# A one-core Mamba block with two adapters: the gate projection and the state sum change places in the pipeline, and the adapters' first projections use four column groups

## The reference, cut to what matters

```python
# 1. adapted projection; A, Bm: the sequence's own rank-16 factors
h0 = x @ W.T + b + 2 * (x @ A) @ Bm
# 2. Mamba mixer, width D = 2048, state size N = 16
u, gate = split(h0 @ W_in.T)              # 2048 + 2048 columns
u = silu(conv4(u) + conv_b)
dt, Bm, Cm = split(u @ Wx.T)              # 64 + 16 + 16, each RMS-normalised
delta = softplus(dt @ Wdt.T + dt_bias)
state = exp(delta * A) * state + delta * u * Bm    # scan over the 256 tokens
y = ((state * Cm).sum(n) + u * D) * silu(gate)
x = x + y @ W_out.T
# 3. second adapted projection, then a mixture of 8 experts of rank 64, top 2
z = x @ base_W.T + base_b + (x @ A2) @ B2
w = top2(softmax(z @ gate_w.T))           # 8 logits for each token
x = x + sum_e w[:, e] * (z @ lora_A[e].T @ lora_B[e].T)
```

## Time and profile before

| | |
|---|---|
| median of three runs | 2683.88 us |
| the profiled execution's own time | 2682.71 us |
| its span | 2680.6 us |
| PE busy | 2405.3 us (90%), 10384 matmul records |
| DVE busy | 2245.6 us (84%) |
| POOL busy | 2118.3 us (79%) |
| ACT busy | 1696.4 us (63%) |
| chain that ended last, by engine | PE 52%, issue 14%, DVE 13%, POOL 10%, ACT 9% |
| DMA | 347.69 MB, mean 130 GB/s |

### The profile page before, as it was taken

How to read it: one execution, slowest core, us unless ns; L and a number is a source line. 1 busy time by engine, 2 the same in 40 slices (tenths; PEclk the granted TensorE clock), 3 DMA queues, 4 the chain that set the end, 5 groups by cost and what they waited for, 6 DMA issues and landing times.

```text
span 2680.6 us, 30841 instructions
## 1 busy us (share of the span) xinstructions
PE 2405.3 (90%) x10384; PEld 1943.0 (72%) x10384; DVE 2245.6 (84%) x2081; ACT 1696.4 (63%) x3754; POOL 2118.3 (79%) x1060
## 2 busy tenths in 40 slices
PE   8987998999989999899989999799989897677979
PEld 6866666677867877687867787688767776566767
DVE  0277788689898989989898989989999999889781
ACT  1366656675677656776577756776577756775450
POOL 0086778689798988989798978898889997999770
PEclk9988999999999999999999999999999998898989
DMA  5452442543354334544244434543345322532331
GB/s 194 124 201 87 110 120 87 160 133 117 125 175 147 126 109 139 169 130 139 91 161 165 134 111 140 174 134 130 104 127 180 126 94 88 175 97 87 110 104 63
DMA packets 115531, 347.69 MB, mean 130 GB/s; under 512 B 21348, under 2 KB 28004, under 8 KB 113902
## 3 DMA queue, kind: packets, MB, share of 16 engines
q1 hardware_dynamic: 92618, 293.80, 33.8%
q10 hardware_dynamic: 22756, 51.92, 5.8%
HBM read 334.66 MB, written 11.02 MB: 129 GB/s over the span
## 4 chain that ended last, share of the span: by engine, by line
PE 52%; issue 14%; DVE 13%; POOL 10%; ACT 9%; ACTq 1%; DMA 0%; SPq 0%; POOLq 0%; DVEq 0%
PE gbank L589 9%; PE ubank L568 9%; DVE scan L1192 8%; PE late L631 6%; POOL st L1397 5%; DVE st L1204 4%; ACT scan L1036 4%; PE small L550 3%; PE late L667 3%; POOL st L1389 3%; PE late L597 3%; PE late L550 3%; ACT L1036 2%; PE small L747 2%; PE late L607 2%
## 5 line engine op out<-in xcount | busy, mean ns | idle before, releaser
L1192 DVE TENSOR_TENSOR_SCAN scan<-scan,st 128x1024 f32<-128x1024 f32 x512 | 1153.3, 2286 | 148.6 <-ACT scan L1036 121.0
L1389 POOL TENSOR_TENSOR st<-w_sb,bc 128x1024 f32<-128x1024 f32 x512 | 1197.2, 2357 | 101.0 <-PE late L597 66.2
L1036 ACT ACTIVATE scan<-delta,A_sb 128x255 f32<-128x255 f32 x2048 | 847.8, 459 | 1.8
L1397 POOL TENSOR_TENSOR st<-st 128x1024 f32<-128x1024 f32 x256 | 603.0, 2355 | 249.0 <-DVE st L1204 238.8
L589 PE MATMUL gbank<-h,wt 128*128 128x256 f32 x2048 | 470.4, 383 | 2.1 <-DMA wt<-in_W_in 2.1
L631 PE MATMUL late<-yg,wt 128*128 128x256 f32 x1792 | 408.6, 387 | 51.6 <-issue 51.6
L1204 DVE TENSOR_TENSOR st<-scan,bc 128x1024 f32<-128x1024 f32 x384 | 453.2, 1208 | 0.0
L589 PEld LDWEIGHTS gbank<-h,wt 128*128 128x128 f32 x2048 | 385.7, 190 | 76.3 <-issue 26.1
L631 PEld LDWEIGHTS late<-yg,wt 128*128 128x128 f32 x1792 | 346.0, 194 | 109.1 <-issue 60.9
L568 PE MATMUL ubank<-h,wt 128*128 128x256 f32 x1712 | 419.6, 402 | 1.3 <-ACT u_sb L903 1.1
L568 PEld LDWEIGHTS ubank<-h,wt 128*128 128x128 f32 x1712 | 350.9, 205 | 59.0 <-ACT u_sb L903 3.0
(11 more groups left out here) (192 smaller groups left out, 2597.2 us busy)
## 6 DMA issues: line engine op xcount, KB each, us to landing
wt<-in_W_in SPq DMA_DIRECT2D x256, 512.0 KB, 3.9
wt<-in_W_out SPq DMA_DIRECT2D x128, 512.0 KB, 3.4
wt<-in_cond_W SPq DMA_DIRECT2D x64, 512.0 KB, 3.7
bc<-bc_rows ACTq DMA_DIRECT2D x64, 512.0 KB, 6.9
wt<-G_tiles SPq DMA_DIRECT2D x32, 512.0 KB, 3.6
wt<-in_ffn_B SPq DMA_DIRECT2D x32, 512.0 KB, 3.4
xb<-in_x SPq DMA_DIRECT2D x8, 1024.0 KB, 5.7
x<-in_x ACTq DMA_DIRECT2D x28, 256.0 KB, 4.0
```

Source lines behind the costliest of these rows:

```text
L1036: last = fn(t[:, k, 1:T], delta[:, c, 1:T], ACT.Exp, scale=A_sb[:, col:col + 1])
L1192: v_.tensor_tensor_scan(Tps[q % 2][:, :], Tps[q % 2][:, :], x_, 0.0, ALU.mult, ALU.add).then_inc(scan_done, 1)
L1389: tt(st[:, n % ST_RING, :, :], w_sb[:, i % 2:i % 2 + 1, :].to_broadcast([P, NQ, T]), bc[:, 0, q * NQ:(q + 1) * NQ, :], ALU.mult).then_inc( ...
L1397: tt(st[:, n % ST_RING, :, :], st[:, n % ST_RING, :, :], st[:, (n - 1) % ST_RING, :, :], ALU.add).then_inc(add_done, 1)
```

## The change

Eight things change, and nothing in what is computed.

1. PE order: `gate_chunk(i+1)` goes to the end of slot i and `sum_states(i-1)` to the start of slot i.
2. The state sum moves from bank late to bank gbank. It waits for the silu of gate i (`q_done`); gate i+1 waits for `y_gate(i-1)`; the folded products of batch 0 (`g`, `b2`, `bias`) wait for `y_gate(i-1)` too. Late jobs no longer wait for `y_gate`.
3. DVE order: `y_sum` and `y_gate` go behind scan 3; `norm` and the first part of softmax stand around scan 2.
4. The jobs of h0 are spread: single chunks in c = 0, 2, 4, 6, 8, 10, two in c = 11, and `la` of sequence b+3 in c = 14. The last `g` job goes to slot 15.
5. Adapters: factor A is padded to 32 columns; part k goes to column group k % 4, so that a bank holds four partial sums on 128 partitions; all 128 rows are copied, and the second factor, held four times at partitions 0, 32, 64, 96 (zeros between), sums them in its matmul.
6. The gate's folded matrix becomes columns 16 to 23 of the second adapter's A, so the logits come from `la2` alone: two matmuls instead of eighteen.
7. Softplus and `delta_add` work on each dt job (two chunks) as it comes, not on pairs.
8. ACT loads a table that holds Exp and Ln right after the gate's silu; dt evacuations all come after `decay(i,3)`.

```diff
@@ late and last jobs, tiles
+    if c == 14 and b + 3 < B:
+        return ("la", b + 3, 0)
...
-        if c == 0:
-            return ("la", j, 0)
-        if c in (1, 3, 5, 6):
-            return ("cond", j, (1, 3, 5, 6).index(c))
-        if c == 8:
-            return ("cond2", j, 4)
+        if c in (0, 2, 4, 6, 8, 10):
+            return ("cond", j, c // 2)
...
+        def softplus_of(i):
+            if i < 0:
+                return []
+            b, c = split(i)
+            if c == 14:
+                return [(b + 1, 0), (b + 1, 1)] if b < LAST else []
+            job = first_job(i)
+            return [job[1:]] if job and job[0] == "dt" else []
@@ SP
-                sp.dma_start(cB[:, :], cond_B[bass.ds(rA, 1)].rearrange("a r o -> r (a o)")).then_inc(cond_ld, 16)
+                for g in range(GR):
+                    sp.dma_start(cB[g * LRG:g * LRG + LR, :], cond_B[bass.ds(rA, 1)].rearrange("a r o -> r (a o)")
+                                 ).then_inc(cond_ld, 16)
@@ PE
                 for k in range(KH):
-                    last = mm(home(job)[0:LR, 0:T], cA[:, k, :], xb[:, k, :], start=(k == 0), stop=(k == KH - 1))
+                    g = k % GR * LRG
+                    last = mm(home(job)[g:g + LRG, 0:T], cA[:, k, :], xb[:, k, :], start=(k < GR), stop=(k >= GR))
...
             def gate_chunk(i):
-                if i:
-                    pe.wait_ge(q_done, i)
-                else:
+                if i == 0:
                     pe.wait_ge(pc_ev, KH + 2)
+                if i >= 2:
+                    pe.wait_ge(yg_done, i - 1)
...
             def sum_states(i):
                 pe.wait_ge(add_done, 3 * i + 3)
+                pe.wait_ge(q_done, min(i + 2, CHUNKS))
-                    last = mm(late[:, 0:T], ident[:, :], st[:, n % ST_RING, k, :], start=(k == 0), stop=(k == 1))
+                    last = mm(gbank[:, 0:T], ident[:, :], st[:, n % ST_RING, k, :], start=(k == 0), stop=(k == 1))
...
-            def logits(f, o):
+            def logits(o):
                 for tc in range(2):
                     tok = slice(tc * P, (tc + 1) * P)
-                    for k in range(KH):
-                        mm(o[:, tc * E:(tc + 1) * E], x_of(f)[:, k, tok], g_gate[:, k, :], start=(k == 0), stop=False)
-                    last = mm(o[:, tc * E:(tc + 1) * E], la2[:, tok], b2g[:, EG:EG + E], start=False, stop=True)
+                    last = mm(o[:, tc * E:(tc + 1) * E], la2[:, tok], b2g[:, EG:EG + E], start=True, stop=True)
...
+            gate_chunk(0)
             for i in range(CHUNKS):
-                gate_chunk(i)
+                if i:
+                    sum_states(i - 1)
                 if first_job(i):
                     run(first_job(i), i)
...
+                if i + 1 < CHUNKS:
+                    gate_chunk(i + 1)
@@ ACT
                 fn(qg[:, i % 2, :], gbank[:, 0:T], ACT.Silu).then_inc(q_done, 1)
-                if job and job[0] not in ("wb", "lg") and in_first_half(job):
+                fn_exp_table()
+                if job and job[0] == "ms":
                     evac(job)
                 decay(i, 2)
...
-                if i in SOFTPLUS_AT:
-                    softplus(*SOFTPLUS_AT[i])
+                for n, j in softplus_of(i):
+                    softplus(n, j)
@@ DVE
                 add_first(i)
+                if b and c == 9:
+                    soft_max_in(b - 1)
+                scan(i, 2)
+                if c == 13 and b < LAST:
+                    norm(b + 1)
+                scan(i, 3)
                 if i:
                     y_sum(i - 1)
...
                     y_gate(i - 1)
-                scan(i, 2)
-                scan(i, 3)
                 mul(i, 2)
                 mul(i, 3)
```

More of the change, by code:

```diff
@@ L25 @@
 LR = 16
+LRG = 32
+GR = P // LRG
 SLOTS = 32
@@ L177, in slot_tiles @@
 def slot_tiles(i):
-    tiles = [("gate", i, 0)]
+    tiles = []
     us = u_chunks(i)
@@ L195, in slot_tiles @@
         tiles += job_tiles(last_job(i))
-    return tiles
-PRO_TILES = [("cond", 0, m) for m in range(KH)] + [("u", v, 0) for v in range(NC)] + [("cond", 1, m) for m in range(4)]
+    if i + 1 < CHUNKS:
+        tiles += [("gate", i + 1, 0)]
+    return tiles
+PRO_TILES = [("cond", 0, m) for m in range(KH)] + [("u", v, 0) for v in range(NC)] + [("cond", 1, m) for m in range(4)] + [
+    ("gate", 0, 0)]
 TAIL_TILES = [("wo3", m, 0) for m in range(PAIRS)] + [("A", LAST, m) for m in range(EK)] + [
@@ L693, in run @@
                     pe.wait_ge(late_ev, LATE_NO[job])
+                    if LATE_NO[job] == 3:
+                        pe.wait_ge(pc_ev, 2 * KH)
+                if kind in ("g", "b2", "bias"):
                     pe.wait_ge(yg_done, i)
-                if kind in ("g", "b2", "bias"):
-                    pe.wait_ge(q_done, i + 1)
                 inc = done_inc(job)
@@ L879, in adapter @@
                 act.wait_ge(*made(job))
-                fn(la[:, :], home(job)[0:LR, 0:T], ACT.Copy, scale=2.0).then_inc(ev_inc(job), 1)
+                fn(la[:, :], home(job)[:, 0:T], ACT.Copy, scale=2.0).then_inc(ev_inc(job), 1)
             def cond_evac(o, j, m):
@@ L906, in x_evac @@
                 act.wait_ge(*made(job))
-                fn(sq[:, :], home(job)[0:RX, 0:T], ACT.Square, bias=one64[:, :]).then_inc(act_step, 1)
-                fn(xs[:, :], home(job)[0:RX, 0:T], ACT.Identity, bias=one64[:, :]).then_inc(ev_inc(job), 1)
+                fn(sq[:, :], home(job)[0:RX, 0:T], ACT.Square, bias=one64[0:RX, 0:1]).then_inc(act_step, 1)
+                fn(xs[:, :], home(job)[0:RX, 0:T], ACT.Identity, bias=one64[0:RX, 0:1]).then_inc(ev_inc(job), 1)
             def ms_evac(job):
@@ L986, in evac @@
                     act.wait_ge(*made(job))
-                    fn(la2[0:LR, :], o[0:LR, 0:T], ACT.Copy).then_inc(ev_inc(job), 1)
+                    fn(la2[:, :], o[:, 0:T], ACT.Identity, bias=one64[:, 1:2]).then_inc(ev_inc(job), 1)
                 elif kind == "A":
@@ L1037, in decay, with fn_exp_table @@
                 last.then_inc(dA_done, 1)
-            def in_first_half(job):
-                return not (job[0] == "dt" and job[2] % 2 == 0 and job[2] >= 2)
+            def fn_exp_table():
+                nc.scalar.preload_act_table_set("natural_log_exp_and_others")
             def softmax_exp(f):
@@ L1066, in _ @@
             softplus(0, 0)
+            softplus(0, 1)
             for q in range(Q):
@@ L1104, in _ @@
                     load_B(b + 1, 3)
-                if job and not in_first_half(job):
+                if job and job[0] in ("dt", "wT"):
                     evac(job)
+                for v in us:
+                    u_evac(v)
                 if i == 0:
@@ L1141, in _ @@
             act.wait_ge(t_la2, 1)
-            fn(la2[0:LR, :], small[0:LR, 0:T], ACT.Copy).then_inc(t_la2, 1)
+            fn(la2[:, :], small[:, 0:T], ACT.Identity, bias=one64[:, 1:2]).then_inc(t_la2, 1)
             for m in range(2):
```

137 lines of the change are left out of this document (61 added, 76 removed).

## The result

The changed kernel takes 2611.88 us (median of 4 runs, 2610.70 to 2612.61) against 2682.51 us of the kernel before on the same chip (2678.38 to 2684.15): ratio 0.9739, 95% interval 0.9722 to 0.9755, 70.6 us less. The forecast was 2608. The profiled execution has a span of 2609.9 us, PE busy 2321.2 (89%), DVE 2239.9 (86%), ACT 1622.4, POOL 2121.8, and 350.04 MB of DMA.

What follows compares the result with a forecast made beforehand. The prediction took DVE as the floor, with late PE orders in a handful of slots above it. Terms -43 - 6 + 4 - 20 - 7 - 4 = -76 on 2682.7 gave 2607, as median 2608 us; range for 8 in 10: 2585 to 2645.

Steps and rivals of the forecast that it cites:

- Batches 2 to 5, -43: Steady batches: 281.1 of DVE work, 11.0 of slot losses and 3.0 for the clock, 295.1 against 305.8, four times.
- c = 10, charged with 2.55: Steady batch, slot c = 10: a cond chunk beside two expert parts makes PE's loop 20.3, a loss of 2.55 us.
- c = 0 and 1, charged with 1.5: Steady batch: c = 0, heavy behind two expert jobs, was to lose 1.5 us.
- The late y pair costs nothing: DVE in each slot: y_sum behind scans 2 and 3 lets the gate start up to 1.25 us late at no cost.
- 1.25 us of free lateness: Each slot: the gate may start as late as 1.25 us into its own slot without delaying scan 2.
- Batch 0, -6: Batch 0: -9 from softplus without loads, +6 from g jobs waiting for y_gate, -3 in slots 14 and 15.
- Slot (1,0), 36: First slot of batch 1: bias, the moved g job, gate and ACT's loads of x lengthen it from 24 to about 36.
- Rival (a): Only the single stalls go, heavy slots keep their loss: 2634, up to 2650 with POOL's 2 a batch; chance 17%.
- Rival (b): PE falls to 1.2 GHz in every slot behind the new waits, and the kernel is slower: about 2700; chance 7%.
- 3.0 a batch for the clock: Steady batches: some 9 us at half speed a batch in or ahead of heavy slots, charged at 3.0.
- Rival (c): The joint table does not save the loads: 11 a batch, seven times, 2684, no gain; chance 5%.
- Rival (d): The adapters' column groups run one after the other: +3, 2611; chance 5%.

Runs made afterwards that it cites:

- e2: The kernel before with the new adapters (four column groups, 128-row second factor, logits in two matmuls) on the old pipeline: 2602.2 us, ratio 0.9723.
- e5: The kernel before with one edit, the state sum ahead of the logits in c = 9 of batches 1 to 7: 2676.4 us, ratio 0.9991.
- e10: The changed kernel with y_sum and y_gate ahead of scan 2 again: 2583.3 us, ratio 0.9641.
- e8: The changed kernel with y_gate wait inside g jobs, last g job in c = 14, la in c = 15, x loads behind decay(16,3): 2601.4 us.
- e3: The changed kernel with all eight matmuls of an adapter in one column group, one after the other: 2622.0 us, ratio 0.9793.
- e9: The changed kernel with the jobs of h0 where they were before and the last g job in c = 14: 2626.3 us, ratio 0.9798.

## Why the forecast held, and where its argument did not

The total came within 4 us and every stage but batch 0 within 6. The reasons behind the largest term were wrong all the same.

- **Batches 2 to 5, -43 (measured -48.5).** Right in size. The forecast credited the late gates' spreading and, for c = 9, "the sum now stands first, the logits are two matmuls". The second half of that sentence did it: c = 9 is 21.40 by the new adapters alone (e2) and 26.10 by the order alone (e5). The spread and the order save time only in part, and softplus for each dt job takes some back. Inside a batch the terms missed one another: c = 10, charged with 2.55, lasts 16.82 and loses nothing, while c = 0 and 1, charged with 1.5, lie 3.7 above DVE's work.
- **The late y pair costs nothing.** Failed. "DVE reaches scan 2 at 8.24 ... since y_sum now stands behind scans 2 and 3" was the ground for 1.25 us of free lateness. e10 shows that the heavy slots keep their length without it and that the delay of y_gate costs 28.6 elsewhere. In the changed kernel a heavy and an easy slot are PE's as a pair: 35.45 busy and two waits of 0.57 make the 36.58, and how late DVE can take a plane does not enter.
- **Batch 0, -6 (measured +7.3): the step that failed by size.** "The loop becomes ... 21.0 in every such slot" held for c = 8 to 11 (21.28). It did not hold for c = 12, 24.65, where the wait for y_gate is followed by PE at its lower clock, nor for c = 7, 23.56. Slots 1 to 5 gave 4.9 (115.7 to 110.8), not 9, and slot 0, which had no term, is 2.3 longer.
- **Slot (1,0), 36 (measured 35.18).** Right, with its steps: bias, g(7), gate, then ACT's evacuations and loads of x. e8 takes 10.9 off it.
- **Rival (a), only the single stalls go.** Nearer to the mechanism than the forecast itself: c = 9 alone gives 6.8 of the 9.0 us that e2 saves in each of batches 2 to 5. Its time (2634 to 2650) was too high; it gave the joint table and the other effects of the adapters nothing.
- **Rival (b), the lower clock in every slot.** It did not come as priced: PEclk stays at 0.97 in batches 2 to 5 and falls from 0.93 to 0.90 in batch 0. But its mechanism is at work in every steady batch. Slots c = 0, 9 and 13 show 0.91, 0.92 and 0.89; behind c = 0 it costs 1.7 to 1.9 (e3, e10), some 7 us over the four batches, and in (0,12) 3 to 4. The forecast's 3.0 a batch for the clock was thus of the right order. One reading under this rival was off: by the earlier trace rows PE is idle for 18% of batches 6 and 7, not for a quarter.
- **Rival (c), the joint table saves nothing.** It was priced at 11 a batch, 77 in all; without the table the kernel loses 128, of it 13.4 in each of batches 2 to 5. The forecast gave the table a gain in batch 0, 6 and 7 and none in the steady batches; it is one of the two sources of the gain: -56 on the old pipeline.
- **Rival (d), the groups run one after the other: +3.** They run side by side, eight matmuls in 1.00 us, where I took 2.0. In one group it is +10, the prologue's two adapters 5.3 of it.

That the sum was right while its main terms had the wrong cause is chance to a good part: gains that were too small for the adapters and the table met losses of the pipeline that were not seen. Undoing one part at a time showed it; the total could not. What stays open: why some waits of PE bring the lower clock and others of nearly the same length do not (in e2 a wait of 3.05 in c = 0 goes with 0.84 in batch 3 and with 1.00 in batches 4 and 5), and how the 5.3 us that e8 has over e9 in slots (0,15) and (1,0) together divide among the moved loads, the order inside the g jobs and the moved `la`; none was tried alone.

## What to carry to other kernels

- Where a change bundles several edits, price each against the kernel before *alone*. Here two edits that touch no order, one of them a single line, give about 135 us, and the reordering around them gives back about 65.
- A wait that names the second of two users of one result is not removed by an order that serves the first: look at what the engine does next (e5), and shorten the result's producer.
- A function table is worth more than its load: the late instruction behind it may be the releaser of another engine. Moving a short operation behind long ones of its engine is priced by who waits for its result, not by what it frees.
- Work taken off PE ahead of a wait can lengthen the wait (2.88 in c = 0 of batch 3, 1.12 in e3), and the matmuls behind it may then run at the lower clock. Compare the granted clock slot by slot before a saving is booked: in e3 the slower adapter made c = 1 shorter by 1.7.

## What was not expected of the hardware

- Four 32-column groups of float32 matmuls overlap almost fully: eight of 256 columns take 1.00 us where they took 3.56 in one group, a factor of 3.6. Two passes at the 0.43 of a 128-column matmul are 0.87 of the 1.00, and of the eight full matmuls on either side (batch 3, c = 8) the ones ahead take 3.54 and the ones behind 3.56 where others take 3.46. The drain at a change of tiling mode that the Trainium skill (TensorEngine Tiling (Array Packing), Key Properties) speaks of can thus be some 0.3 here for both changes together, where the prediction took 0.4. The 1.5 us that the prediction estimated from the Trainium skill's TensorE: Matmul & The Clock Gate (rules for small-M) was too long.
- The instruction that asks for the joint table costs nothing beyond the load that stood there: 128 loads of 1283 ns, one in each slot, and Ln and Exp follow without another.
- A wait of 3.82 us on PE was followed by 6.36 us at the lower clock for work that takes 3.60 at the upper one: with the matmuls of eight columns in between, the wait's price came to 7.4, 1.9 times its length. In c = 0 of the steady batches waits of 2 to 3 us did the same on a smaller scale.
